# A fused GNN, linear-attention and expert layer on one core: sums taken two steps behind the keys, biases in a weight's column, and a tile's last group begun ahead of its branches

## What is computed

```python
xn  = layernorm(x)                                   # x: 6250 x 512
agg = segment_sum(xn[src], dst) / max(degree, 1)     # 16 edges a node on average
gnn = xn @ W1.T + b1 + agg @ W2.T + b2
q, k, v = relu(xn @ Wq.T), relu(xn @ Wk.T), xn @ Wv.T          # 16 heads of 32
att = q @ (k.T @ [v, 1]) per head, divided by its last column  # linear attention
x2  = x + gnn + att @ proj.T + proj_b
g   = gate(attention_pool(layernorm(x2)))            # two of eight experts chosen
out = x2 + sum_e g[e] * gelu(gelu(layernorm(x2) @ w1[e] + b1[e]) @ w2[e] + b2[e])
```

## Time and profile before

| | us |
|---|---|
| median of 3 runs | 1630.05 (1627.26 to 1630.59) |
| the profiled execution | 1630.57 |
| its span, first to last instruction | 1628.8 |
| k loop, first K matmul to last G matmul | 23.6 to 322.6 |
| first gather that waits for PE to the last gather | 337.5 to 1313.3 |
| rest | 1313.4 to 1628.8 |
| PE busy, whole span | 1522.9 (93%) |
| POOL busy, whole span | 842.2 (52%) |
| mean granted PE clock | 0.982 of full speed |

### The profile page before, as it was taken

How to read it: one execution, slowest core, us unless ns; L and a number is a source line. 1 busy time by engine, 2 the same in 40 slices (tenths; PEclk the granted TensorE clock), 3 DMA queues, 4 the chain that set the end, 5 groups by cost and what they waited for, 6 DMA issues and landing times.

```text
span 1628.8 us, 29257 instructions
## 1 busy us (share of the span) xinstructions
PE 1522.9 (93%) x7546; PEld 732.1 (45%) x7547; DVE 1064.1 (65%) x2216; ACT 608.7 (37%) x997; POOL 842.2 (52%) x873
## 2 busy tenths in 40 slices
PE   4899899979999999999999999999999989999997
PEld 2444344434444444444444444444444444444443
DVE  8677522256767676667666667666666666677667
ACT  5777622212333333333333333333333344555554
POOL 3345350057777777777777777777777710000000
PEclk8999999999999999999999999999999998999999
DMA  9967672247777777777777777777777723222223
GB/s 289 235 175 177 139 174 46 72 141 226 238 233 227 227 234 229 233 235 235 226 234 232 236 230 234 235 233 231 234 236 233 236 89 124 74 97 96 96 101 115
DMA packets 165342, 308.82 MB, mean 190 GB/s; under 512 B 70378, under 2 KB 72964, under 8 KB 165036
## 3 DMA queue, kind: packets, MB, share of 16 engines
q0 software_dynamic: 62720, 205.57, 43.0%
q1 hardware_dynamic: 34912, 59.68, 11.1%
q10 hardware_dynamic: 67660, 42.96, 10.4%
HBM read 255.80 MB, written 39.49 MB: 181 GB/s over the span
## 4 chain that ended last, share of the span: by engine, by line
PE 63%; POOL 10%; issue 6%; DMA 4%; DVE 2%; ACT 0%; DVEq 0%; SPq 0%; ACTq 0%; POOLq 0%
PE bank L539 13%; PE bank L540 13%; PE bank L544 13%; POOL ring L512 10%; PE bank L612 8%; PE bank L613 8%; DMA ring<-table,src_col 3%; PE bank L793 1%; PE bank L699 1%; PE bank L701 1%; PE bank L700 1%; PE bank L752 1%; PE bank L759 1%; DMA xT<-xT 1%; DVE ring L1530 1%
## 5 line engine op out<-in xcount | busy, mean ns | idle before, releaser
L512 POOL DMA_INDIRECT ring<-table,src_col x784 | 752.0, 959 | 344.5 <-issue 230.3
L612 PE MATMUL bank<-ring,onehot 128*128 x830 | 316.4, 381 | 46.0 <-issue 31.5
L613 PE MATMUL bank<-ring,onehot 128*128 x830 | 316.1, 381 | 0.0
L539 PE MATMUL bank<-wts,xT 128*128 128x512 f16 x588 | 225.7, 384 | 15.8 <-DMA xT<-xT 8.9
L540 PE MATMUL bank<-wts,xT 128*128 128x512 f16 x588 | 225.9, 384 | 0.0
L1190 DVE TENSOR_TENSOR onehot<-bank,dst_col 128x512 f32 x244 | 168.8, 692 | 38.0 <-DVE bank L1184 31.5
L544 PE MATMUL bank<-wts,xT 128*128 128x512 f16 x588 | 152.2, 382 | 0.0
L539 PE MATMUL bank<-wts,work 128*128 128x512 f16 x392 | 150.1, 383 | 0.0
L540 PE MATMUL bank<-wts,work 128*128 128x512 f16 x392 | 150.0, 383 | 0.0
L612 PEld LDWEIGHTS bank<-ring,onehot 128*128 x830 | 80.9, 97 | 153.8 <-issue 76.0
L915 ACT ACTIVATE work<-bank,rd 128x512 f32<-128x512 f32 x49 | 33.7, 687 | 303.0 <-DVE rd L1201 240.6
(11 more groups left out here) (273 smaller groups left out, 2636.4 us busy)
## 6 DMA issues: line engine op xcount, KB each, us to landing
ring<-table,src_col POOLq DMA_INDIRECT x784, 3.8
x_rows<-work ACTq DMA_DIRECT2D x49, 256.0 KB
work<-in_x ACTq DMA_DIRECT2D x48, 256.0 KB
ring<-x_rows SPq DMA_DIRECT2D x12, 1024.0 KB, 5.3
out_x<-ring SPq DMA_DIRECT2D x12, 1024.0 KB
table<-xT SPq DMA_DIRECT2D x46, 256.0 KB, 2.2
ring<-in_x SPq DMA_DIRECT2D x42, 256.0 KB, 2.8
xT<-in_L_mix_qkv_weight SPq DMA_DIRECT2D x2, 1024.0 KB, 10.1
```

The source lines that it names most:

```text
L512: pool.indirect_dma_start(ring[:, n, :], None, table[:, :], bass.IndirectOffsetOnAxis(ap=ap, axis=0)).then_inc(slot_loaded[n], 16)
L539: mm(out_, wh(c), mh(c), start=first and c == 0, stop=False)
L612: mm(ps_agg[:, :], w[:, k, :], rows[:, k, 0:D], start=start, stop=False, skip_group_check=True)
L613: r = mm(ps_agg[:, :], w[:, k, :], rows[:, k, D:2 * D], start=False, stop=stop, skip_group_check=True)
```

## The change

The k loop: PE does G(i-2) first and K(i) after it, where it did K(i) and then G(i-1). There are three buffers for the high and low keys (`khl`) in place of two and three semaphores for the transposes. `OFF` and `NS` go from 3 to 4, `LEAD` from 6 to 4, `KP` from 28 to 26. On ACT a step is now prepare, transpose, the two key reads, normalize; it was normalize, prepare, the two reads, transpose. Within one normalization ACT takes the root of the next tile ahead of the high part, and DVE takes the next mean ahead of the low part. `kacc` is gone: the last column of every natural row is a constant, so the sum of k stands in the last row of G and is read out by `last_row` after the value product.

Biases: they are loaded by output row (`bcol`, 128 x 4 elements each) right after the weights, summed on POOL and written by ACT into the last column of the raw W1 in place of zero. The matmul adds them; `xb` and L1411 are gone. `x_in` enters the sum directly and serves as scratch for the score product.

DMAs: a transfer of 106 rows goes as 96 and 10 rows (`parts`). The weights Wq, W1 and W2 are asked for at t = 8, 11, 14 (were 7, 9, 11), the edges from 17 on (was 14). Wq gets its scale in its own step, and the scale for W1 and W2 in step 10.

The last group of a tile does block 0 first, without a condition, then 1, 2 and 3 under nested branches, and a one-column matmul at the end raises the semaphore.

```diff
-NS = 3
+NS = 4
-OFF = 3
-LEAD = 6
+OFF = 4
+LEAD = 4
-KP = 28
+KP = 26
+STEPS[10].append(("scale", 1))
-    n = LEAD + (3 * (i + 1) + 1) // 2
-    return range(n, min(LEAD + (3 * (i + 2) + 1) // 2, T + 2))
+    n = LEAD + 3 * (i + 1) // 2
+    return range(n, min(LEAD + 3 * (i + 2) // 2, T + 2))
+def parts(n):
+    whole = n // 16 * 16
+    return [(0, n)] if whole == n else [(0, whole), (whole, n)]
...
@@ sync
+                for k, b in enumerate((gb1, gb2, proj_b)):
+                    sp.dma_start(bcol[:, k], b.rearrange("(a p) -> p a", p=P)).then_inc(s["biases_loaded"], 16)
-                    sp.dma_start(xin[0:n, t % XI, :], x[t * P:t * P + n, :]).then_inc(x_loaded[t % XI], 16)
-                if t == 7:
+                    for a, b in parts(n):
+                        sp.dma_start(xin[a:b, t % XI, :], x[t * P + a:t * P + b, :]).then_inc(x_loaded[t % XI], 16)
+                if t == 8:
                     weight(WQ, qkv_w[0:D])
...
@@ gpsimd
+            pool.wait_ge(s["biases_loaded"], 48)
+            link(pool.tensor_tensor(out=bcol[:, 0], in0=bcol[:, 0], in1=bcol[:, 1], op=ALU.add))
+            pool.tensor_tensor(out=bcol[:, 0], in0=bcol[:, 0], in1=bcol[:, 2], op=ALU.add).then_inc(s["biases_added"], 1)
             for k in (WV, WQ):
                 pool.wait_ge(w_loaded[k], 16)
...
-                pool.tensor_tensor(out=khl[i % 2][:, D:2 * D], in0=k32, in1=khl[i % 2][:, 0:D],
+                pool.tensor_tensor(out=khl[i % 3][:, D:2 * D], in0=k32, in1=khl[i % 3][:, 0:D],
                                    op=ALU.subtract).then_inc(s["klo_made"], 1)
-                after(pool, s["kacc_made"], i)
-                pool.tensor_tensor(out=kacc, in0=kacc, in1=k32, op=ALU.add).then_inc(s["kacc_made"], 1)
...
@@ tensor
                 if part == "last":
-                    with pe.If(f >= 2):
-                        when(f >= 3, 3)
-                        add(2)
-                    when(f >= 1, 1)
-                    add(0).then_inc(s["oh_used"], 1)
+                    add(0)
+                    with pe.If(f >= 1):
+                        add(1)
+                        with pe.If(f >= 2):
+                            add(2)
+                            when(f >= 3, 3)
+                    nothing().then_inc(s["oh_used"], 1)
                     return
...
+                t = i - 2
+                if t >= 0:
+                    pe.wait_ge(s["klo_made"], t + 1)
...
                 if 0 <= i < T:
-                    pe.wait_ge(turned[i % 2], 16 * (i // 2) + 16)
+                    pe.wait_ge(turned[i % 3], 16 * (i // 3) + 16)
...
-                t = i - 1
-                if t >= 0:
-                    pe.wait_ge(s["klo_made"], t + 1)
...
-            pe.wait_ge(s["kacc_made"], T)
-            pe.wait_ge(s["khi_made"], T - 1)
-            for c in range(C):
-                mm(ps_deg[:, 8 + c:9 + c], kacc[:, c * P:(c + 1) * P], ones[:, 0:1], start=True, stop=True)
-            mm(bank[4][:, :], ones[:], kacc, start=True, stop=True).then_inc(s["ksum_made"], 1)
...
             r.then_inc(s["vt_made"], 1)
+            for c in range(C):
+                mm(ps_deg[:, 8 + c:9 + c], gt32[3][:, c * P:(c + 1) * P], ident[:, P - 1:P], start=True, stop=True)
+            mm(bank[4][:, :], last_row, gt32[3], start=True, stop=True).then_inc(s["ksum_made"], 1)
...
@@ scalar
             for i in range(-1, T):
-                for n in norm_slots(i):
-                    normalize(n)
                 for kind, c in STEPS.get(i, ()):
                     prepare(done, kind, c)
                     done += 1
...
                 if i >= 0:
+                    turn(i + 2)
                     act.wait_ge(s["k_made"], i + 1)
                     after(act, s["klo_made"], i)
-                    after(act, s["kacc_made"], i)
                     F(k32, k_bank(i)[:, :], ACT.Relu, scale=SK).then_inc(s["k32_made"], 1)
-                    after(act, s["g_made"], i - 1)
+                    after(act, s["g_made"], i - 2)
...
-                    turn(i + 2)
+                for n in norm_slots(i):
+                    normalize(n)
+                if i in (4, 6):
+                    k = {4: G1, 6: G2}[i]
+                    less_last(raw_w[k], (w_loaded[k], 16), s["weights_ready"], bcol[:, 0, :, None] if k == G1 else None)
...
@@ vector
                     after(dve, s["x2_stored"], 16 * t)
-                    after(dve, s["xb_made"], t + 1)
-                    V.scalar_tensor_tensor(out=x2, in0=ps_o[:, :], scalar=mix[:, 1:2], in1=xb,
+                    after(dve, s["x_loaded2"], 16 * t + 16)
+                    V.scalar_tensor_tensor(out=x2, in0=ps_o[:, :], scalar=mix[:, 1:2], in1=x_in,
...
-                t = i - 1
-                if real(t):
-                    after(dve, s["x_loaded2"], 16 * t + 16)
-                    after(dve, s["sraw_made"], t)
-                    V.tensor_tensor(xb, x_in, biasb[:], ALU.add).then_inc(s["xb_made"], 1)
```

More of the change, by code:

```diff
@@ L178, in program @@
         work = sb("work", [P, 12, D], F32)
-        wvT, gt32 = work[:, 0:4], work[:, 4:8]
+        wvT, gt32 = work[:, 0:4], [work[:, k] for k in (4, 5, 6, 7)]
+        last_row = work[:, 8, 0:P]
         vtm = work[:, 0].rearrange("p (a f) -> p a f", a=C)
         diag_m, diag_end = work[:, 1, 0:P], work[:, 11, 0:2 * P]
-        k32, khl, kacc = work[:, 4], [work[:, 5 + b].bitcast(F16) for b in range(2)], work[:, 7]
-        x2, xn2, acc, pT_, x_in, w32, xb, ahT_ = (work[:, k] for k in range(8))
+        k32, khl = work[:, 4], [work[:, b].bitcast(F16) for b in (5, 6, 8)]
+        x2, xn2, acc, pT_, x_in, w32, _, ahT_ = (work[:, k] for k in range(8))
         ah = work[:, 8:12]
@@ L287, in program @@
         slot_loaded = [ctx.enter_context(nc.semaphore(f"slot_loaded{k}")) for k in range(R)]
-        turned = [ctx.enter_context(nc.semaphore(f"tile_turned{k}")) for k in range(2)]
+        turned = [ctx.enter_context(nc.semaphore(f"tile_turned{k}")) for k in range(3)]
         block = ctx.enter_context(nc.Block())
-        NCONST = 13
+        NCONST = 12
         def natural(t):
@@ L360, in _ @@
             weight(WV, qkv_w[2 * D:3 * D])
+            with nc.allow_non_contiguous_dma(reason="three biases by output row, 6 KB in all"):
+                for k, b in enumerate((gb1, gb2, proj_b)):
+                    sp.dma_start(bcol[:, k], b.rearrange("(a p) -> p a", p=P)).then_inc(s["biases_loaded"], 16)
             for t in range(XI, T + XI):
@@ L387, in _ @@
                 stored(sp, r - NS)
-                sp.dma_start(table[r * P:r * P + n, :], natural(r)[0:n, :]).then_inc(row_stored[r % NS], 16)
+                for a, b in parts(n):
+                    sp.dma_start(table[r * P + a:r * P + b, :], natural(r)[a:b, :]).then_inc(row_stored[r % NS], 16)
             sp.wait_ge(s["firsts_made"], 1)
@@ L677, in _ @@
             n = 0
-            for i in range(-1, T + 1):
+            for i in range(-1, T + 2):
                 for kind, c in STEPS.get(i, ()):
@@ L874, in normalize @@
                       ).then_inc(s["xn_made"], 1)
+                if n < T:
+                    act.wait_ge(s["mv_made"], n + 1)
+                    F(std2[:, n % 2], mv2[:, n % 2, 1:2], ACT.Sqrt, bias=epsc[:], scale=1.0 / (SX * SX)
+                      ).then_inc(s["std_made"], 1)
+                if 0 <= t < T:
                     if RAW[WK] <= t + OFF < RAW[WK] + C:
@@ L923, in turn, with less_last @@
                     stored(act, t - OFF)
[L924 to L926 removed]
+                    act.dma_start_transpose(xT[:, t, :, :], natural(t)).then_inc(turned[t % 3], 16)
+            def less_last(raw, done, sem, instead=None):
                 act.wait_ge(*done)
@@ L935, in less_last @@
                     F(raw[:, a, 0:D - 1], raw[:, a, 0:D - 1], ACT.Identity, bias=last[:, a:a + 1])
+                if instead is not None:
+                    act.wait_ge(s["biases_added"], 1)
+                    F(raw[:, :, D - 1:D], instead, ACT.Copy).then_inc(sem, 1)
+                    return
                 F(raw[:, :, D - 1:D], raw[:, :, D - 1:D], ACT.Copy, scale=0.0).then_inc(sem, 1)
```

208 lines of the change are left out of this document (96 added, 112 removed).

## The result

The changed kernel takes 1612.18 us (median of 4 runs, 1610.02 to 1613.50), against 1630.32 before (4 runs): ratio 0.9882, 95% interval 0.985 to 0.9914. Forecast were 1604 and a range of 1594 to 1618. A second series of the same kernel gave 1609.71 against 1631.21 (6 and 11 runs, ratio 0.987, 0.9844 to 0.9895). The gain is 18.1 us in the first series and 21.5 in the second, where 26 were forecast. All executions told of here are fast ones but the profiled one of run 4 (1953.0 us where its median is 1936.71), so of that profile only the k loop is read.

The account below looks back on a forecast made before the run. POOL bounds the layers, PE with its waits the k loop, ACT's serial work the start. Start -13, loop -11, turn +0.6, gather -2.4 make -25.8 from 1630.57, less 0.5: 1604 us, range 1594 to 1618 (8 in 10).

Parts of the forecast that it names:

- the turn: Between the k loop's end and the first released fetch: net +0.6 us, from -1 to +2.
- The start: Up to K(10): K(10) starts at 85.6 to 88 instead of 99.51, -13 us, from -10 to -16.
- the sum of ACT's work: Start of the loop: reads, normalizations, weight copies and subtractions total 40.6 us on ACT, ending at 83, and set K(10).
- The three bias loads: SP's queue at the start: up to 12 us together, from about 12 to 24, hidden, 0.
- The loop's -11: K loop behind K(10): of 12.8 us of waits about 2 stay, -11, from -7 to -12.
- G(i-2) needs a low key made one whole step earlier: K loop: with one POOL operation a tile, PE's low-key wait (4.9 us, 7 times) goes too.
- Rival C: K loop: the transpose's issue blocks ACT, whose step becomes 6.8 us against PE's 5.62; +9, 1639 us; chance 0.05.
- The gathers' -2.4: Gathers in the layers: removing L1411 saves 2.4 us on 24 slow fetches, from 0 to -7.2; slow fetches fall to about 39.
- The rule by which I split the fetches: Gathers: only a DVE operation under way at a fetch's start costs it; 2.4 us for L1411.
- the fetch of 407.31: Gathers: took 1.14 us, 0.20 too long, though L1411 began only after it; 22 others with this excess stay.
- rival A: Gathers and start: fetches gain the whole 7.2 us of overlap and the start goes at ACT's floor; 1597 us; chance 0.15.
- The last group's order: Layers: the new order is on PE only, which has 47 us in hand: 0.

Follow-up runs that it names:

- run 4: Changed kernel with the first low key on POOL made ahead of the subtraction on Wq: 1936.71 us, ratio 0.997 to before.
- Run 3: Changed kernel with the two scale entries (steps 6 and 10) done at the end of their step on PE and DVE: 1929.73 us, ratio 0.9953 to before.
- run 1: Changed kernel with G one step back in code, K(i) then G(i-1): 1933.55 us, ratio 0.9968 to before.
- run 2: Changed kernel with the transfers of 106 rows whole again, not split into 96 and 10: 1937.37 us, ratio 0.9995 to before.
- run 10: Changed kernel with a second POOL operation for each of the first 27 tiles, ACT's next key read waiting for it: 1944.74 us, ratio 0.9993 to before.
- Run 9: Changed kernel with transposes asked for behind the step's key reads, and only when G(i-1) is done: 1974.46 us, ratio 1.0148 to before.
- run 6: Changed kernel with K(i) then G(i-1) and the first low key ahead of the subtraction on Wq: 1604.06 us, ratio 0.9829 to before.
- run 7: Changed kernel with one more two-input VectorE sum a tile, at the place and size of L1411: 1616.70 us, ratio 0.9908 to before.
- run 11: Changed kernel with one more single-input VectorE operation a tile (bn_stats of x_in, 0.69 us): 1947.40 us, ratio 1.0019 to before.

## Why the prediction was right and where it was not

**The sign, the range and the larger part of the mechanism held.** The k loop gives nearly all of the gain, behind K(10) no wait of PE over 0.3 us is left, POOL stays the limit of the gathers, the turn costs 0.3.

**The start was mis-sized: -13 forecast, -6.1 measured** (-7.5 in the second series, with K(10) at 92.03). The first half of the time axis was right: K(2) was put at 39 to 41 and came at 39.73, and G(0) waited for the low key behind Wq till 35.74 (35.5). The step that failed is the sum of ACT's work as the only limit up to K(10). PE kept its own pace, 5.6 us a step, and K(9) came at 83.1; what was missing is a term for the two scale entries. Each stands right behind its step's weight block, so PE reaches it before ACT or DVE has done the copy of the step before (61.67 and 88.85 in the first fence). At 61.67 that copy had itself stood behind ACT's subtraction on W1 (58.49 to 61.05): the forecast had this work in ACT's total, but no place where PE would stop for it. Behind each wait the granted clock is half for 3.4 us, from 62.5 and from 89.8, and matmuls are 0.43 us from start to start, where 0.22 is the full one. Steps 6 and 10 took 9.7 and 10.3 us. Before, with PE later, this same wait was 0.38 once. Run 3 shows that 3.3 us of it can be had back, and run 1 that 5.7 can, by moving the weight block, each to 1 or 2 us. The three bias loads held SP's queue for 9.1 us, from 2.9 to 12.0 and not from 12 to 24, and are hidden as forecast.

**The loop's -11 came as -12.8, partly for a wrong reason.** That all 12.8 us went is more than forecast: nothing stayed. But "G(i-2) needs a low key made one whole step earlier" is not so: the series of matmuls is the same as before (run 1). What doubled is only a transpose's lead. The old code asked behind G(i-1), 5 us ahead of K(i+2); the new one with a fourth natural row asks behind G(i-2), before the reads, 10 us ahead (208.20 for a K at 218.2). Before, the 12.8 us behind K(10) were 6.9 of waits for transposes, 2.2 for low keys, 0.7 for copies of a block, and about 3 of slower matmuls behind the gaps. For the transposes the earlier request is enough: with a landing of 9.08 us and a lead of 10.03 run 2 has no wait, where a landing of 10.52 and a lead of about 5.2 gave the wait of 5.33 before. The split of the 106 rows isn't needed for that, though only 1 us is in hand without it. What took away the low keys' 2.2 us is not shown: the lighter POOL isn't needed (run 10), which leaves ACT's new order and the third key buffer, both untested. Run 9 undid the request in a form that did more harm than the old code.

**Rival C did not come, and its price was seen elsewhere.** Issuing a transpose took 1.25 us beside running instructions and cost ACT nothing in most steps. It blocks ACT where the issue itself is slow: ACT stood 3.8 us behind one of 5.2 in run 6.

**The gathers' -2.4 came as -1.1 to -2.2.** The rule by which I split the fetches, that only an operation under way at the fetch's start costs, is borne out by run 7, and it costs until 0.13 before its end. It has two limits: the operation must have begun some 0.1 us ahead of the fetch, and not every operation costs (run 11). The prediction left the fetch of 407.31 unexplained. L1401, a sum with two inputs, ran under it from 406.89 to 407.64, so it ended 0.33 after the fetch's start, and the 0.20 follows by the same rule. By my count now the 24 fetches under L1411 were 2.6 us too long, not 2.4. The number of slow fetches was not as forecast: 47 and 42 in place of 39. L1401 held up 23 before and holds up 27 and 20 now (it is L1411 of the changed kernel), two others held up 12 and now 15 and 19, and one that had held up none, L1324, now 3 and 3, since the operations moved in time. The full overlap of rival A (7.2) is excluded for this change.

**The last group's order** was put at 0 and stays open between 0 and 4 us.

**The best version** is run 6, 1604.06 us, ratio 0.9829 to before. Its interval (0.9801 to 0.9857) just meets that of the changed kernel (0.9844 to 0.9895); the earlier first fetch, by 5.1 us, speaks for the difference of 5.7.

## What to carry to other kernels

Write the series of instructions out before you believe in a longer pipeline: a loop that says i-2 can issue the same order as one that said i-1, and what changed is only what moved past it. Every extra entry in a step of a two-deep exchange between engines brings it one step closer to its producer, and in a start-up that is where the wait falls. When a change makes one stage earlier, list what now meets it there: weight loads, the queue that issues transposes, and the clock behind each gap. And when an engine waits for a transfer, count the requests to find the one that it waits for: the one that looks worst in the timeline may belong to a later tile.

## What the runs showed of the hardware

- A gather's instruction on GpSimd, 0.94 us, is held up by a VectorE sum with two SBUF inputs that began 0.09 us or more ahead of it, until 0.13 us before the sum ends (1.42 us beside one that ended 0.60 in). It is not held up by a `bn_stats` of the same length. A `tensor_scalar` with one input row held it up too, if it had begun 0.17 us or more ahead (run 11). Where the sum began less than 0.05 ahead, the sum was the longer one, 0.73 to 0.77 in place of 0.69.
- Three chips ran the same programs. On one the kernel before takes 1631 us, on two 1943 and 1946. The mean granted clock is 0.90 to 0.92 there in place of 0.98. The page's row of one group of matmuls in the layers, first of the changed kernel and then of run 1, shows where PE stops:

```profile
L545 PE MATMUL bank<-wts,work 128*128 128x512 f16 x392 | 148.3, 378 | 0.0
```

```profile
L545 PE MATMUL bank<-wts,work 128*128 128x512 f16 x392 | 165.6, 422 | 67.9 <-issue 67.0
```

  67 us of idle time before it, released by nothing that the program waits for. What it is stays open; a 1% change could be told on the first of them alone.
- The issue of a DMA transpose takes 1.25 us in most steps, and 3.8 to 5.2 three times near loads of 1 MB. It landed 3.7 us after the request in the median of the kernel before, and up to 14.2 after it at the start of the loop. Beside a transfer of 106 rows it was 9.1 and 10.5, and 4.0 where that went as 96 and 10.
